# Layer 1's experts padded to 256 rows instead of 512, and two intermediate results kept on chip

## The reference

```python
def reference(...):
    x = L0_attn_x                                   # 8 x 512 rows of 256, float32
    xn = _layernorm(x, axis=-1)
    s = _L0_attn_ref(xn, ...)                       # layer 0 mixer: q, k, v; cumulative sums; gates; + xn
    g = _silu(_L0_ffn_ref(xn, ...))                 # 16 experts; each takes its 64 best of 512 rows
    x = x + s * g
    xn = _layernorm(x, axis=-1)
    s = _L1_attn_ref(xn, ...)                       # 16 heads of 16, softmax over 512 rows, + its normed input
    g = _silu(_L1_ffn_ref(xn, ...))
    x = x + s * g
    return x

    # _L1_ffn_ref: 8 experts of 256 x 512 x 256, each row goes to its best two, and a shared expert
        _, idx = jax.lax.top_k(logits + rb, K)
        w = jax.nn.softmax(gathered, axis=-1)
        h = jnp.einsum('bsd,edh->bseh', x, W1) * jax.nn.silu(jnp.einsum('bsd,edh->bseh', x, W3))
        expert_out = jnp.einsum('bseh,ehd->bsed', h, W2)
        out = jnp.einsum('bsed,bse->bsd', expert_out, w_full)
        hs = jnp.einsum('bsd,dh->bsh', x, Ws1) * jax.nn.silu(jnp.einsum('bsd,dh->bsh', x, Ws3))
        out = out + jnp.einsum('bsh,hd->bsd', hs, Ws2)
```

## Time and profile before

| | us |
|---|---|
| median of three runs | 1905.79 (1901.66 to 1905.82) |
| profiled execution, its own time | 1906.22 |
| its span, first to last instruction | 1904.5 |
| mixer and experts of layer 0 | 104 to 650 |
| preparation of layer 1 | 661 to 816 |
| attention stage: start, first exponential, last exponential, last instruction | 846, 886, 1841, 1850 |
| finish | 1857 to 1904 |

### The profile page before, as it was taken

How to read it: one execution, slowest core, us unless ns; L and a number is a source line. 1 busy time by engine, 2 the same in 40 slices (tenths; PEclk the granted TensorE clock), 3 DMA queues, 4 the chain that set the end, 5 groups by cost and what they waited for, 6 DMA issues and landing times. The chain is left out here.

```text
span 1904.5 us, 24624 instructions
## 1 busy us (share of the span) xinstructions
PE 1618.3 (85%) x8530; PEld 1101.8 (58%) x8530; DVE 1172.0 (62%) x1868; ACT 894.2 (47%) x1420; POOL 666.7 (35%) x645
## 2 busy tenths in 40 slices
PE   4448999999999559925999999999999999999960
PEld 3326777777777436612566666666666666666630
DVE  4436556755675356565666676767677666767614
ACT  2124544554455233211545456565656566665632
POOL 2222442544354255303132312443443433344320
PEclk8669999999999879966999999999999999999995
DMA  5344446644552379833233243545445454544318
GB/s 163 127 133 99 106 103 158 152 114 103 153 120 69 63 242 360 310 110 108 84 112 106 96 139 105 134 114 134 125 110 139 103 134 110 139 114 120 84 23 264
DMA packets 214026, 251.61 MB, mean 132 GB/s; under 512 B 19344, under 2 KB 164240, under 8 KB 213904
## 3 DMA queue, kind: packets, MB, share of 16 engines
q1 hardware_dynamic: 185296, 212.73, 36.5%
q0 software_dynamic: 28608, 37.31, 11.6%
HBM read 153.34 MB, written 96.10 MB: 131 GB/s over the span
## 5 line engine op out<-in xcount | busy, mean ns | idle before, releaser
L1565 ACT ACTIVATE a_prob<-a_score_bank 128x1024 f32<-128x1024 f32 x256 | 262.9, 1027 | 358.9 <-PE a_score_bank L1440 256.3
L1670 DVE TENSOR_REDUCE a_neg_max<-a_max_bank 128x2 f32<-128x1024 f32 x256 | 312.3, 1220 | 118.5 <-PE a_max_bank L1423 117.7
L1384 POOL DMA_INDIRECT fs<-a_y,a_token x92 | 143.4, 1558 | 182.5 <-ACT a_y L1605 159.4
L1450 PE MATMUL a_bank<-a_prob,a_va 128*32 128x512 f32 x1024 | 137.2, 607 | 22.5 <-DVE a_ml L1679 20.0
L1423 PE MATMUL a_max_bank<-a_ka,a_qa 48*128 48x512 f32 x512 | 132.4, 514 | 27.9 <-DVE a_neg_max L1670 17.3
L1693 DVE SCALAR_TENSOR_TENSOR a_tg<-a_tg,a_bank 128x512 f32<-128x512 f32 x124 | 84.8, 684 | 95.1 <-ACT a_tg L1575 91.5
L653 POOL DMA_INDIRECT f<-e_ye,c_slot_row x64 | 100.9, 1577 | 73.4 <-issue 49.6
L1440 PE MATMUL a_score_bank<-a_qa,a_ka 50*128 50x512 f32 x512 | 106.6, 412 | 4.1 <-ACT a_prob L1565 4.1
L1423 PEld LDWEIGHTS a_max_bank<-a_ka,a_qa 48*128 48x128 f32 x512 | 49.2, 189 | 100.0 <-DVE a_neg_max L1670 42.4
L427 PE MATMUL e_bank<-m_wqkv,m_xnT 128*128 128x512 f32 (+1 forms) x256 | 91.1, 500 | 16.2 <-DVE e_qkv L681 14.8
L741 DVE TENSOR_TENSOR e_h<-e_bank,e_sge 128x512 f32<-128x512 f32 x64 | 44.2, 691 | 85.8 <-ACT e_sge L565 85.2
(11 more groups left out here) (319 smaller groups left out, 4401.5 us busy)
## 6 DMA issues: line engine op xcount, KB each, us to landing
a_raw<-in_W SPq DMA_DIRECT2D x69, 512.0 KB, 4.2
e_raw<-in_w SPq DMA_DIRECT2D x48, 512.0 KB
a_qa<-qk SPq DMA_DIRECT2D x192, 64.0 KB
a_ka<-qk SPq DMA_DIRECT2D x192, 64.0 KB
xs<-c_pad SPq DMA_DIRECT2D x23, 516.0 KB
a_xg<-xs SPq DMA_DIRECT2D x23, 516.0 KB, 7.1
qk<-p_hi SPq DMA_DIRECT2D x32, 256.0 KB, 5.8
qk<-p_lo SPq DMA_DIRECT2D x32, 256.0 KB, 5.5
```

What stands on the lines that cost most here:

```text
L1384: nc.gpsimd.indirect_dma_start(f_rows, bass.IndirectOffsetOnAxis(token[x % 4][:, t:t + 1], 0), y[:, t, :], None, compute_op=ALU.add).then_ ...
L1450: ins = nc.tensor.matmul(OB[rows, :], va[g % NR][:, j, rows], prob[j % 2][:, h_, :], start=j == 0, stop=j == T - 1, tile_position=(0, 32 * ...
L1565: nc.scalar.activation(prob[j % 2][:, 2 * p:2 * p + 2, :], S2[:], ACT.Exp, scale=float(D) ** -0.5).then_inc(p_done, 1)
L1670: nc.vector.tensor_reduce(neg_max[:, g % 2, :, T * p + t], M[:], AX.X, ALU.max, negate=True).then_inc(mx_done, 1)
```

## The change

It has three parts.

- **Half groups.** `GS` is 256. An expert's rows are padded to 256, and two half groups, with an owner each, make one group of 512 in one turn: `NG` = 40 half groups, `NX` = 20 groups, `NF` = 28. Each group of layer 1's own experts now needs two weight sets, which go alternately to the two places of the hi and lo tiles. An up chunk (`chunk`) covers two 128-wide parts of the hidden width and 256 rows, where it covered one part and 512 rows; so its matmuls are 128 x 256 and twice as many, for the shared expert too. `down` takes the second half's w2 from tile 2 on. Turns 28 to 31 have no up work, turn 28 has the last `down`.
- **The mixer's result on chip.** `k.rows`, 32 KB in each partition, holds first the transposed normed input of layer 0 (`m.xnT` is a view of it), then batch for batch the mixer's result, then what `k.xa_all` held. The scratch tensor `s0`, its 8 stores and 8 loads are gone.
- **x1 in free weight tiles.** At the end of the attention stage SP loads `x1` into eight tiles of `raw` and of place 0 of the weights. `finish` loads only `fs`, up to four batches ahead.

Cut to its core:

```diff
-GS = 512
-NG = (NTOK * TOP + E1 * (GS - 1)) // GS
+GS = 256
+NG = ((NTOK * TOP + E1 * (GS - 1)) // GS + 1) // 2 * 2
+NX = NG * GS // S
...
                 if kind == "turn":
-                    sp.wait_ge(s0_out, 16 * a)
-                    sp.dma_start(s0[:], at(xn_b, a)).then_inc(xres_in, 16)
-                elif kind == "out":
-                    sp.wait_ge(s0_done, a + 1)
-                    sp.dma_start(at(s0_b, a), s0[:]).then_inc(s0_out, 16)
+                    sp.wait_ge(qkv_ps, T * (a + 1))
+                    sp.wait_ge(xres_in, 16 * a)
+                    sp.dma_start(k.rows[:, a], at(xn_b, a)).then_inc(xres_in, 16)
...
-            sp.wait_ge(s0_out, NB * 16)
-            sp.wait_ge(filled, (NG + 1) * 16)
+            sp.wait_ge(filled, (NX + 1) * 16)
...
                 for i in range(2):
-                    part = s0[:, 2 * i:2 * i + 2, :].rearrange("p t d -> p (t d)")
+                    part = k.rows[:, n, 2 * i:2 * i + 2, :].rearrange("p t d -> p (t d)")
...
-                for buf, src in ((f0, f0_b), (s0, s0_b), (x, x_b)):
+                for buf, src in ((f0, f0_b), (x, x_b)):
                     sp.dma_start(buf[u][:], at(src, n)).then_inc(x_in[u], 16)
...
+    NF, HC = NB + NX, FC // 2
+    assert 2 * GS == S and NF <= G - 1
...
-    def weights(e):
-
-        return max(e - NB + 1, 0)
+    def weights(e, s):
+
+        return 2 * (e - NB) + s + 1 if e >= NB else 0
+
+    def place(v):
+
+        return (v + 1) % 2
+
+    def used(v):
+
+        return NB + (v - 1) // 2, (v - 1) % 2
+
+    NW = weights(NF - 1, 1) + 1
+
+    def chunk(c):
+
+        s, fp = divmod(c, HC)
+        return slice(2 * fp, 2 * fp + 2), slice(s * GS, (s + 1) * GS)
...
             for g in range(G):
                 e = g
-                v = weights(e + 1)
-                fresh = v and group(e + 1)
                 if g + 2 < G:
                     load_qk(g + 2)
                 store(e - 2, 1)
-                if fresh:
-                    load_w(0, v)
-                    load_w(1, v)
                 if group(e + 1):
                     load_x(e + 1)
+                if NB <= e + 1 < NF:
+                    load_w(0, weights(e + 1, 0))
+                    load_w(1, weights(e + 1, 0))
                 if g + 2 < G:
                     load_v(g + 2)
+                if NB <= e < NF:
+                    load_w(2, weights(e, 0))
                 if g + 1 < G:
                     max_rows(g + 1)
                 store(e - 1, 0)
-                if fresh:
-                    load_w(2, v)
+                if NB <= e + 1 < NF:
+                    load_w(0, weights(e + 1, 1))
+                    load_w(1, weights(e + 1, 1))
+                if NB <= e < NF:
+                    load_w(2, weights(e, 1))
...
             sp.wait_ge(fs_out, 2 * NB * 16)
+            sp.wait_ge(up_ps, FC * NF)
+            sp.wait_ge(y_ps, 2 * NF)
+            for b in range(NB):
+                sp.dma_start(k.x1[b], at(x1_b, b)).then_inc(k.x1_in, 16)
+            sp.wait_ge(k.x1_in, NB * 16)
...
@@ -1393,6 +1415,9 @@
                     scatter_rows(e + 1)
                 if NB <= e - 2 < NF:
                     combine(e - 2 - NB, 1)
+                if NB <= e < NF:
+                    low_w(0, weights(e, 1))
+                    low_w(1, weights(e, 1))
                 if NB <= e + 1 < NF:
                     marks(e + 1 - NB)
...
                 if NB <= e + 1 < NF:
-                    low_w(0, weights(e + 1))
-                    low_w(1, weights(e + 1))
-            pool.wait_ge(f_out, 16 * GT * NG)
+                    low_w(0, weights(e + 1, 0))
+                    low_w(1, weights(e + 1, 0))
...
+            def up(bank, w, e, c):
+                v = weights(e, c // HC)
+                fs, rows = chunk(c)
+                for i, f in enumerate(range(fs.start, fs.stop)):
+                    ins = product3(nc, bank[:, i * GS:(i + 1) * GS], w[place(v)], xT,
+                                   [((slice(None), d, slice(f * P, (f + 1) * P)), (slice(None), d, rows)) for d in range(DC)])
+                return ins
+
+            def up_gate(e, c):
+                if c % HC == 0:
+                    pe.wait_ge(w31_lo, 2 * weights(e, c // HC) + 2)
...
+                if t % 2 == 0:
+                    pe.wait_ge(w2_lo, v + 1)
...
-                    ins = product3(nc, YB[:, (t % 2) * D:(t % 2 + 1) * D], hT[e % 2], w2[weights(e) % 2],
+                    ins = product3(nc, YB[:, (t % 2) * D:(t % 2 + 1) * D], hT[e % 2], w2[place(v)],
...
+                fresh = NB <= e < NF
+                coming = NB <= e + 1 < NF
                 exps(g, 0)
                 if group(e - 2):
                     weighted(e - 2, 1)
                 if group(e):
                     tanh(e, 0)
+                if fresh:
+                    high_w(0, weights(e, 1))
 
                 exps(g, 1)
                 if g:
                     copy_o(g - 1)
                 if group(e):
                     high_h(e, 0)
+                if fresh:
+                    high_w(1, weights(e, 1))
 
                 exps(g, 2)
-                if e == 0 or NB <= e < NF:
-                    high_w(2, weights(e))
+                if e == 0:
+                    high_w(2, 0)
+                if NB <= e - 1 < NF:
+                    high_w(2, weights(e - 1, 1))
                 if group(e):
...
                     weighted(e - 1, 0)
+
                 exps(g, 4)
                 if group(e):
                     tanh(e, 2)
+                if coming:
+                    high_w(0, weights(e + 1, 0))
 
                 exps(g, 5)
                 if group(e):
                     high_h(e, 2)
-                if NB <= e + 1 < NF:
-                    high_w(0, weights(e + 1))
+                if coming:
+                    high_w(1, weights(e + 1, 0))
 
                 exps(g, 6)
-                if NB <= e + 1 < NF:
-                    high_w(1, weights(e + 1))
                 if group(e):
                     tanh(e, 3)
+                if fresh:
+                    high_w(2, weights(e, 0))
...
-            weighted(NF - 1, 1)
...
+                if e == 0:
+                    low_w2(0)
                 if group(e):
                     hidden(e, 1)
                 maxima(g + 2, 0)
                 if group(e):
                     low_h(e, 1)
                 split_max(g + 1)
+                if NB <= e - 1 < NF:
+                    low_w2(weights(e - 1, 1))
                 maxima(g + 2, 1)
...
                     low_h(e, 3)
+                if NB <= e < NF:
+                    low_w2(weights(e, 0))
...
-    fs, x1 = [[sb(f"{n}{u}", [P, T, D]) for u in range(2)] for n in ("fs", "x1")]
+    fs = [sb(f"fs{b}", [P, T, D]) for b in range(NB)]
+    AHEAD = 4
...
             def load(b):
-                sp.dma_start(fs[b % 2][:], at(fs_b, b)).then_inc(in_[b % 2], 16)
-                sp.dma_start(x1[b % 2][:], at(x1_b, b)).then_inc(in_[b % 2], 16)
-
-            load(0)
-            load(1)
+                sp.wait_ge(in_[b % AHEAD], 16 * (b // AHEAD))
+                sp.dma_start(fs[b][:], at(fs_b, b)).then_inc(in_[b % AHEAD], 16)
+
+            for b in range(AHEAD):
+                load(b)
             for b in range(NB):
+                if b + AHEAD < NB:
+                    load(b + AHEAD)
                 sp.wait_ge(y_done, b + 1)
-                if b + 2 < NB:
-                    load(b + 2)
                 sp.dma_start(at(out_b, b), y[b % 2][:]).then_inc(y_out[b % 2], 16)
...
-                nc.vector.tensor_tensor(flat(s2[u][:]), flat(k.xa_all[:, b]), flat(g[u][:]), ALU.mult).then_inc(s2_done, 1)
+                nc.vector.tensor_tensor(flat(s2[u][:]), flat(k.rows[:, b]), flat(g[u][:]), ALU.mult).then_inc(s2_done, 1)
                 dve.wait_ge(s2_done, b + 1)
                 if b >= 2:
                     dve.wait_ge(y_out[u], 16 * (b // 2))
-                dve.wait_ge(in_[u], 2 * 16 * (b // 2 + 1))
-                nc.vector.tensor_tensor(flat(y[u][:]), flat(s2[u][:]), flat(x1[u][:]), ALU.add).then_inc(y_done, 1)
+                nc.vector.tensor_tensor(flat(y[u][:]), flat(s2[u][:]), flat(k.x1[b]), ALU.add).then_inc(y_done, 1)
...
+        k.rows = Room(nc, whole, "x_").sb("rows", [P, NB, T, D])
...
+            m.xnT = k.rows[:].rearrange("p b (c h) d -> p b c (h d)", c=DC)
...
+        late = Room(nc, whole, "late_")
+        k.raw = [late.sb(f"raw{i}", s) for i, s in enumerate(([P, DC, FF], [P, DC, FF], [P, FC, D]))]
+        k.w3, k.w1, k.w2 = [[[late.sb(f"{n}{u}{part}", s, F32R) for part in ("hi", "lo")] for u in range(2)]
+                            for n, s in (("w3", [P, DC, FF]), ("w1", [P, DC, FF]), ("w2", [P, FC, D]))]
+        k.x1_in = late.sem("x1_in")
+        u = 0
+        flat = [k.raw[0][:], k.raw[1][:], k.raw[2][:], *(part[:].bitcast(F32) for part in (*k.w3[u], *k.w1[u], k.w2[u][0]))]
+        k.x1 = [ap.rearrange("p a f -> p (a f)").rearrange("p (t d) -> p t d", d=D) for ap in flat]
```

124 lines of the change are left out of this document (59 added, 65 removed).

## The result

The changed kernel takes 1921.5 us (median of 4 executions, 1912.7 to 1924.6) against 1905.8 for the kernel before (median of 4, 1901.7 to 1905.8): a ratio of 1.008, 95% interval 1.0043 to 1.0118. It is slower by 0.8%, where 1853 us and a ratio of 0.972 were forecast. The profiled execution took 1912.7 us, with a span of 1910.9. It is the fastest of the four; the others show a mean granted clock of 0.906 to 0.910 where it shows 0.916, and have no trace. All that follows explains 1912.7, not the 9 us from there to the median.

What follows compares the result with a forecast made beforehand. TensorE's own work bounds most stretches, data the finish; -40 + 9.5 + 2 + 0 - 2 - 6 - 17.5 = -54 from 1906.2, stated as 1853 us; forecast 1846 to 1861 (0.61), range 1840 to 1876.

Steps and rivals of the forecast that it cites:

- three groups fewer: Turns 28 to 31, losing group work: 65 us in place of 105.3, so -40 us.
- 256-column products: Up and gate matmuls cut from 512 to 256 columns, twice as many: +0.34 us a turn.
- second set and split: Turns 8 to 27: second weight set per group +2 us (0 to 10), 256-column matmuls +7.
- up to the first exponential: Layer 1's preparation, one DMA load of three less: -2 us (0 to -6).
- gap to the finish: From last exponential to finish, 15.9 us before: last scatter gone, addition ends earlier, -6 us (-4 to -9).
- the finish: Final stage, x1 already on chip: 29.7 us in place of 47.2, so -17.5 us (-14 to -19).
- rival 3: Group turns: GpSimd's late subtractions hold up a VectorE subtraction of h; up to 2.4 us a turn, 1901 us; chance 0.04.
- rival 1: Bare turns at the end: TensorE's clock falls, -28 us in place of -40, 1865 us; chance 0.13.
- +5.2 for down pieces: Turn 28 keeps four down pieces of 1.6 us, some in slack: +5.2 us, so 21.5 us.
- The split: 256-column up and gate matmuls in 28 group turns: +9.5 us by the rows, +3.4 by the Trainium skill's formula.
- SP's queue: Group turns: q and k loads queue behind a new wait but land with 1.6 us of slack, so 0.

Runs made afterwards that it cites:

- e1: Changed kernel with both GpSimd subtractions for the second weight set waiting for the turn's first low_h: 1871.8 us, ratio to before 0.981.
- e5: Changed kernel with only the second of GpSimd's two subtractions waiting for the turn's first low_h: 1873.0 us, ratio to before 0.984.
- e4: Changed kernel with filler matmul products without use in turns 28 to 31: 1923.1 us, ratio to before 1.007.
- e10: Changed kernel with both GpSimd subtractions after the first low_h, GpSimd's addition later, q/k loads ahead of the second w2 load: 1857.2 us, ratio 0.974.
- e9: Changed kernel with both GpSimd subtractions after first low_h, tail weighing sets ahead of score pairs, later addition, filler products in turns 28 to 31: 1860.8 us, 0.975.
- e7: Changed kernel with both GpSimd subtractions after the first low_h and GpSimd's addition behind the turn's second scatter: 1866.3 us, ratio 0.980.
- e14: Changed kernel, GpSimd subtractions after first low_h, weighing sets ahead in tail, later addition, q/k ahead of w2, filler only in turns 29 to 31: 1851.6 us, 0.971.
- e12: Kernel before with only GpSimd's addition moved behind the second scatter of the turn: 1902.8 us, ratio 0.998.
- e3: Kernel before with three added GpSimd subtractions a group turn, each waiting for the one ahead: 1996.2 us, ratio 1.046.
- e2: Changed kernel with GpSimd's two subtractions for the second weight set replaced by memsets of the same tiles: 1872.9 us, ratio 0.983.

## Why the prediction was wrong, point by point

Against the profiled executions, 1906.2 and 1912.7:

| step | forecast | measured |
|---|---|---|
| turns 28 to 31, three groups fewer | -40 | 105.3 to 82.1: -23 |
| 256-column products, turns 0 to 7 | +0.34 a turn | 242.6 to 243.1: +0.06 a turn (over all traces +0.23) |
| turns 8 to 27: second set and split | +2 and +7 | 30.39 to 33.41 in 18 turns: +54 |
| up to the first exponential | -2 | 886.0 to 884.4: -1.6 |
| gap to the finish | -6 | 15.9 to 10.06: -5.9 |
| the finish | -17.5 | 47.2 to 29.3: -17.9 |
| sum | -54 | +6 |

**The step that failed** is the sentence on the second weight set: "None becomes the bound by sum; the question is place." The loads by sum were right (VectorE 22.3 us a turn in e1), and the question was put. But the places were then worked out for ScalarE's copies, for VectorE's two w2 subtractions and for SyncE's queue, and not for GpSimd's two new subtractions: outside rival 3 their wait was put at nothing, and the +2 us of the second set are for VectorE's w2 subtraction. They cost the greater part of the 54: 33.41 - 30.88 = 2.5 us in each of 18 turns by e1, 45 us. The order of the change has them behind the scatter of the group two turns back. In the kernel before, in turn 20, which starts at 1493.30, GpSimd's timeline has the last issue of that scatter, and VectorE's the first `low_h`:

```profile
1497.78 1.55 POOL L1384 DMA_INDIRECT fs<-a_y,a_token  x1 [0.30 <-issue]
```

```profile
1499.08 0.69 DVE L1701 TENSOR_TENSOR a_hT0lo<-a_h,a_hT0hi 128x512 fp32r<-128x512 f32 x1 [0.90 <-ACT a_hT0hi L1581]
```

What GpSimd does next starts some 1.0 us after such an issue by its records (1526.39 to 1527.38 in the changed kernel), so at 1498.8 here, 0.3 us ahead of `low_h`. That the two come together in every turn, within half a microsecond, could have been read off the trace of before.

**Rival 3** was this mechanism at 0.04. Its place and its condition were wrong: it asked that the subtractions "run late by 1.7 us" to meet the second `low_h`; at the first one no lateness was needed. That its price was near (2.4 us a turn forecast at the most, 3.0 measured) is luck. It let `low_h` wait for one subtraction of 2.39 us and charged all of it, and by e5 one costs 0.1 to 0.3 us a turn. `low_h` waits for both, as there is no gap between them, and two cost 2.5. The rule of the Trainium skill that the prediction cites beside it speaks of one instruction that blocks; here there were two in a row, and the trace shows VectorE shut out for both.

**Three groups fewer.** Here two terms failed. The first is the clock: the bare turns were priced at 1.00 and were granted 0.88 to 0.60, which is rival 1, and its -28 was nearer than the forecast, at -23 measured. In turn 31 it is 2.8 of the 3.2 us by which 16.4 exceeds the forecast 13.2, by the estimate beside e4. The second is the step: 1.65 us was taken for each step without maxima, from a row of a step with no weighing set in it. Four of eight steps have one, and at full clock one of these four takes 2.69. In turn 31 that is 1.0 us more, of which the forecast gave back 0.6 by counting eight steps where there are seven and an exponential. Turn 28's +5.2 for down pieces left out the q/k loads, 3.9 us late there; its turn is 29.0, and 25.8 with them in time (e10). What makes turns 29 and 30 longer than forecast at full clock (19.5 and 16.5 us in e9, for 16.3 and 13.8) stays open.

**The split** was costed at 0.34 us a turn by two spacings, the smaller of them of the down products. In turns 10 to 27 of the changed kernel the split products themselves start 0.118 us apart in the median, and the unsplit ones before 0.231: 48 x (2 x 0.118 - 0.231) = 0.24 us a turn. Turns 0 to 7 have no second set. They are 0.06 us a turn longer by the two profiled executions, but that difference is within what such numbers repeat: by the mean of the thirteen traces with the split (242.4 to 246.4 us for eight turns) and the three without (241.1 to 242.6) it is 0.23. So the rows' price was 0.1 us a turn too high. The sentence behind it, by the Trainium skill's page "TensorE: Matmul & The Clock Gate" (Back-to-back issue gap), gave +3.4 us in all, 0.12 a turn, as much too low; the page gives that formula for a single matmul in isolation.

**SP's queue**, put at 0 with 1.6 us of slack, was late in turns 10 to 27 once `low_h` was repaired, by 0.7 us in the turn of e7 shown and up to 1.2 in others. Two terms were too small. The landing of 64 KB, estimated as half of a 512 KB piece's, 2.1 us, measured 3.3 to 3.8. And the twelve issues took 6.7 us for 5.3, so that they ended 1391.89 + 3.83 - 1387.77 = 7.95 us into the turn, 1.4 later than forecast. It did not show in the result of turns 10 to 27 because rival 3's wait covered it. It showed in turn 28, where e10 gains 4 us; in turns 10 to 27 e10 gains 6.

**Right as forecast:** the gap and the finish, 23.8 us together for 23.5, and by the steps that were named: the addition ends 5.4 us after the last exponential (4.4 forecast) and 4.7 more go by (5); in the finish VectorE starts 4.9 us in (5.8), is at it for 21.0 (20.2) and the last store takes 3.4 (3.7). Turns of a second set need not be longer: 30.28 us in e14, with the addition moved, against 30.23 in e12. The start's 1.6 us can't be counted as a hit: the first exponential comes at 883.3 to 888.6 us in the traces with the change and at 885.3 to 887.9 in those without.

**The range.** 1840 to 1876 was built around one failure at a time. With e1's one wait the kernel is in it (1871.8), and with five edits it takes the forecast time (1851.6). That agreement is luck: in e14's trace turns 28 to 31 are 12 us above the forecast's 65, and the 20 turns with a second set some 11 below it, partly by a gain that was no part of the forecast (the addition, some 4 us).

## What to carry to other kernels

An engine's sum of busy time says that new work fits and nothing about what it meets. Write down, for each added operation, when its inputs are there and what stands ahead of it in its queue, and lay that against the operations of the engine it shares an interface with, in every turn and not at the one place already known to collide. Two short collisions in a row can cost many times what one does, because the first uses up the slack. And when one wait is repaired, look for the one that it covered: here the q/k loads behind the late `low_h`. When work is added to hold a clock up, look where it stands: filler in the chain that it is to speed up can spend all that the clock gives back, and the total then reads as if the clock didn't matter.

## What the runs showed of the hardware

- A VectorE subtraction with two SBUF inputs that comes while GpSimd runs SBUF-reading subtractions without a gap isn't let in between them: 5.55 us on average behind two, 3.21 behind one, 0.69 behind none or beside memsets. Where each GpSimd operation waited for the one ahead, VectorE got in behind the first (e3: 3.2 us, with three of them queued).
- GpSimd's subtraction is recorded longer too when VectorE wants in: 2.97 us each in the changed kernel's turn 20, 2.39 undisturbed.
- Products with 256 columns start 0.118 us apart in the median, those with 512 columns 0.231 (turns 10 to 27 of the changed kernel and of the one before): 48 more of them cost 0.24 us a turn.
- TensorE's granted clock was 1.00 throughout turns 10 to 26 in e1 and 0.97 in the changed kernel, where TensorE stands 2.3 us or more in each of them. In the last turn it was 1.00 in the kernel before and 0.60 in the changed one. With the same code there it was 0.50 in e1, e2 and e5 and 0.73 in e7, and the turn lasted 17.8 and 15.1 us for 16.4.
